# Router logits from the first norm's transposed rows and eight extra projection columns, in place of the second norm's transposes

## The reference

```python
h = patches(x) @ W_lin.T + b_lin, with class token and positions; then the text rows
h = h + attention(layernorm(h))          # Wq, Wk, Wv, causal, every fourth key left out, Wp
z = layernorm(h)
xn = z * rsqrt(mean(z * z) + 1e-5) * norm_weight
logits = xn @ router_w.T + router_b
probs = softmax(logits)
gates, idx = top_k(probs.T, T_all // 8)  # each expert picks its tokens
h = h + sum over experts of gates * (gelu(xn[idx] @ fc1.T + b1) @ fc2.T + b2) / sum of gates
```

## Time and profile before

| | |
|---|---|
| runs, median of 3 | 848.52 us (846.49 to 848.92) |
| the profiled execution | 851.07 us, span 849.0 us |
| granted TensorE clock, mean | 0.929 |
| PE busy | 748.5 us (88%), 6840 matmuls |
| PE weight loads busy | 675.5 us (80%) |
| DVE busy | 567.4 us (67%) |
| ACT busy | 398.0 us (47%) |
| POOL busy | 383.7 us (45%) |

### The profile page before, as it was taken

One profiled execution on the slowest core, in us unless ns is written; L12 is line 12 of the kernel. 1 busy time (PEld: TensorE's weight loads), 2 busy tenths in 40 slices (PEclk: granted clock), 3 DMA queues, 4 the chain that ended last, 5 costly groups with the idle time before them and its releaser, 6 DMA issues. The chain is left out here.

```text
span 849.0 us, 18781 instructions
## 1 busy us (share of the span) xinstructions
PE 748.5 (88%) x6840; PEld 675.5 (80%) x6840; DVE 567.4 (67%) x1343; ACT 398.0 (47%) x857; POOL 383.7 (45%) x534
## 2 busy tenths in 40 slices
PE   6788999999999999999999521379999999999994
PEld 5667888888888888888887421379999999999994
DVE  1245867668667677677675267785787787877561
ACT  0314445454455454454542247045547466375570
POOL 4223455364464454554542426023636437355334
PEclk9899999999999999999998755569999999999998
DMA  9965477465774566666653162112344443443122
GB/s 308 272 99 89 56 116 114 88 87 98 107 117 92 89 102 93 123 107 95 90 95 71 36 216 65 40 28 82 41 132 78 106 141 53 129 98 35 36 30 32
DMA packets 80583, 82.37 MB, mean 97 GB/s; under 512 B 35705, under 2 KB 73575, under 8 KB 80236
## 3 DMA queue, kind: packets, MB, share of 16 engines
q1 hardware_dynamic: 65964, 62.21, 37.5%
q0 software_dynamic: 11840, 11.12, 8.3%
q10 hardware_dynamic: 2688, 7.85, 3.3%
HBM read 34.59 MB, written 16.22 MB: 60 GB/s over the span
## 5 line engine op out<-in xcount | busy, mean ns | idle before, releaser
L625 POOL DMA_INDIRECT out<-r_arena x48 | 80.0, 1666 | 117.9 <-DVE r_arena L1582 106.0
L529 POOL TENSOR_SCALAR_AFFINE_SELECT r_arena<-r_arena 126x660 f32<-126x660 f32 x128 | 97.5, 771 | 59.1 <-ACT r_arena L687 58.6
L687 ACT ACTIVATE r_arena<-ps_all 126x660 f32<-126x660 f32 x128 | 92.3, 721 | 67.2 <-PE ps_all L915 66.0
L1289 DVE TENSOR_REDUCE mx<-ps_all 128x4 f32<-128x504 f32 (+1 forms) x160 | 105.0, 668 | 24.3 <-PE ps_all L892 23.1
L1300 DVE RECIPROCAL r_arena<-ps_all 128x165 f32<-128x165 f32 x64 | 76.1, 1189 | 56.3 <-PE ps_all L930 56.3
L915 PE MATMUL ps_all<-Qp,Kp 98*126 98x166 f32 x512 | 85.6, 291 | 9.9 <-DMA Qp<-mT 6.9
L892 PE MATMUL ps_all<-Kp,Qp 96*65 96x56 f32 (+1 forms) x512 | 93.5, 298 | 0.0
L1604 DVE TENSOR_TENSOR hT_lo<-r_arena,hT_hi 128x330 fp32r<-128x330 f32 x128 | 63.3, 500 | 40.3 <-ACT r_arena L794 40.3
L612 POOL DMA_INDIRECT xe<-xn_rows,r_arena x48 | 60.3, 1256 | 59.7 <-issue 35.7
L792 ACT ACTIVATE hT_hi<-ps_all,vec_s 128x330 fp32r<-128x330 f32 x128 | 69.1, 540 | 36.1 <-PE ps_all L1157 34.0
L1157 PE MATMUL ps_all<-xeT_hi,W_hi 128*128 128x330 f32 x256 | 83.4, 326 | 1.1 <-DVE xeT_lo L1596 1.1
(11 more groups left out here) (181 smaller groups left out, 1712.7 us busy)
## 6 DMA issues: line engine op xcount, KB each, us to landing
H<-w SPq DMA_DIRECT2D x16, 1024.0 KB, 5.9
Qp<-q_hi SPq DMA_DIRECT2D x64, 166.0 KB, 3.9
Kp<-k_hi SPq DMA_DIRECT2D x128, 63.0 KB, 4.1
Qp<-q_lo SPq DMA_DIRECT2D x32, 166.0 KB, 4.7
out<-H SPq DMA_DIRECT2D x16, 330.0 KB
xn_rows<-r_arena SPq DMA_DIRECT2D x16, 330.0 KB
H<-h ACTq DMA_DIRECT2D x13, 336.0 KB, 23.5
Kp<-k_lo SPq DMA_DIRECT2D x64, 63.0 KB, 4.1
```

The source lines that it names most:

```text
L529: pool.affine_select(PT[0:S, g, :, :], PT[0:S, g, :, :], [[0, 4], [STEP - 1, T]], ALU.is_ge, 0.0, base=STEP - 2, channel_multiplier=-STEP) ...
L625: pool.indirect_dma_start(rows_out, bass.IndirectOffsetOnAxis(tok[0:A, e % NTB, a:a + 1], 0), yw[0:A, a, :], None, bounds_check=NTOK - 1, ...
L687: act.activation(PT[0:S, g, :, :].rearrange("p (k h) t -> p k h t", k=2), pair[:, :, :, 0:T], ACT.Exp, scale=float(HD) ** -0.5).then_inc(e ...
L1289: dve.tensor_reduce(dst, src, AX.X, ALU.max).then_inc(max_ready, 1)
```

## The change

The logits are linear in the residual stream before its norms' scales: h after attention is (first norm's rows) / rs + bias rows + y @ Wp. G is router_w times norm_weight with each expert's mean over the 256 inputs taken away, so that the second norm's shift drops out. `route(n)` now multiplies xnT, the first norm's transposed rows of pair n, by G; it is issued in the even round, two to three rounds ahead of the projection, into unused columns of bank 2. `router_part` on DVE scales that by the first norm's spread and adds a constant, into eight columns that every token row of H gets (U). Eight columns Wp @ G are put behind the projection's weights, so `project` writes 264 columns and `residual` adds the router's part with the rest. `logits(p)` on POOL multiplies U by the second norm's scale and adds the bias. `transposes2`, `copy_xn2T` and `copy_logits` go; xn2 is still made and stored, as the experts gather it. Round 33 of PE's list goes. `router_mean`, `router_projection`, `router_bias` and their DVE parts set up the constants in rounds -1 to 1. The bank waits of `queries` and `keys` that named `copy_xn2T` or the logits now name xnT.

```diff
+DL = D + NE
 BIG0 = T - 128
 SMALL = 65
+SCRATCH = 2 * T + 6
...
-        H = sb("H", [128, NT * D])
-        H4 = H[:, :].rearrange("p (n r d) -> p n r d", n=NPAIR, r=RT)
+        H = sb("H", [128, NT * DL])
+        HL = H[:, :].rearrange("p (n r d) -> p n r d", n=NPAIR, r=RT)
+        H4, U = HL[:, :, :, 0:D], HL[:, :, :, D:DL]
...
-            W_s = sb1("W_s", [128, 4, KD, D])
...
+            W_p, W_pT = sb1("W_p", [128, KD, DL]), sb1("W_pT", [128, KD, D])
+            bpe = sb1("bpe", [128, DL])
+            bvB, bpB = sb1("bvB", [128, KD, A]), sb1("bpB", [128, KD, A])
...
+                if n >= 3:
+                    pool.wait_ge(u_ready, RT * (n - 2))
+                    apart(pool)
+                pool.tensor_tensor(spread[0:A, n % 3, :], vv[0:A, :], rs[0:A, :], ALU.mult).then_inc(spread_ready, 1)
...
+                if p == NPAIR - 1:
+                    logits(p)
                 pool.tensor_tensor(shift2[0:A, :], shift2[0:A, :], rs2[0:A, :], ALU.mult).then_inc(shift2_ready, 1)
+
+            def logits(p):
+                if p == 0:
+                    pool.wait_ge(row_in, 16)
+                    apart(pool)
+                mine = L[0:A, RT * p:RT * p + RT, :]
+                scale = rs2[0:A, :].rearrange("p (r o) -> p r o", o=1).to_broadcast([A, RT, NE])
+                bias = rb_s[0:A, :].rearrange("p (o e) -> p o e", o=1).to_broadcast([A, RT, NE])
+                pool.tensor_tensor(mine, U[0:A, p], scale, ALU.mult).then_inc(scaled, 1)
+                pool.wait_ge(scaled, p + 1)
+                apart(pool)
+                pool.tensor_tensor(mine, mine, bias, ALU.add).then_inc(logit_ready, 1)
             def norm_weight(p):
                 if p >= 2:
                     pool.wait_ge(xn_stored[p % 2], 16 * (p // 2))
                     apart(pool)
-                    pool.wait_ge(t2_done, 2 * p - 2)
...
+                if p < NPAIR - 1:
...
+                    logits(p)
...
+            act.dma_start(W_p[:, :, 0:D], watt[:, 3]).then_inc(w_in, 16)
...
+            act.dma_start(W_pT[:, :, :], wpT).then_inc(wpT_in, 16)
...
-            def copy_xn2T(p):
...
+            act.wait_ge(xn2_ready, RT * NPAIR)
...
+                if c == 0 and b >= 1:
+                    pe.wait_ge(u_ready, RT * min(b // 2 + 2, NPAIR))
+                if c == 1 and b <= 1:
+                    pe.wait_ge(router_ready, 3 + b)
...
             def project(p, r, free):
                 if r == 0:
                     pe.wait_ge(yT_ready, 4 * p + 4)
+                    pe.wait_ge(router_ready, 3)
                 pe.wait_ge(*free)
                 for k in range(KD):
-                    mm = pe.matmul(bank(project_bank(p, r))[0:A, 0:D], yT[:, p % 2, k, r * A:(r + 1) * A], W_p[:, k, :],
+                    mm = pe.matmul(bank(project_bank(p, r))[0:A, 0:DL], yT[:, p % 2, k, r * A:(r + 1) * A], W_p[:, k, :],
 ...
-            def transposes2(p, c, free):
...
-            def route(p):
-                pe.wait_ge(xn2T_ready, 2 * p + 2)
+            def router_mean():
+                pe.wait_ge(router_ready, 1)
+                for k in range(KD):
+                    mm = pe.matmul(bank(3)[:, SCRATCH:SCRATCH + NE], kf("ones")[:, 0:128], G[:, k, :],
+                                   start=(k == 0), stop=(k == KD - 1))
+                mm.then_inc(router_sum, 1)
+
+            def router_projection():
+                pe.wait_ge(wpT_in, 16)
+                pe.wait_ge(router_ready, 2)
+                for c in range(KD):
+                    for k in range(KD):
+                        mm = pe.matmul(bank(3)[:, SCRATCH + (c + 1) * NE:SCRATCH + (c + 2) * NE],
+                                       W_pT[:, k, c * 128:(c + 1) * 128], G[:, k, :],
+                                       start=(k == 0), stop=(k == KD - 1))
+                mm.then_inc(router_sum, 1)
+
+            def router_bias():
+                pe.wait_ge(bvB_ready, 1 + KD)
+                pe.wait_ge(router_ready, 3)
+                dst = bank(3)[0:A, SCRATCH + 3 * NE:SCRATCH + 4 * NE]
+                for k in range(KD):
+                    pe.matmul(dst, bvB[:, k, :], W_p[:, k, D:DL], start=(k == 0), stop=False)
+                for k in range(KD):
+                    mm = pe.matmul(dst, bpB[:, k, :], G[:, k, :], start=False, stop=(k == KD - 1))
+                mm.then_inc(router_sum, 1)
+
+            def route(n):
+                pe.wait_ge(router_ready, 2)
+                pe.wait_ge(xnT_ready, 2 * n + 2)
+                if n >= 2:
+                    pe.wait_ge(u_ready, RT * (n - 1))
+                at_col = SCRATCH + n % 2 * RT * NE
                 for r in range(RT):
                     for k in range(KD):
-                        mm = pe.matmul(bank(7)[0:A, r * NE:(r + 1) * NE], xn2T[:, k, r * A:(r + 1) * A], rw_s[:, k, :],
+                        mm = pe.matmul(bank(2)[0:A, at_col + r * NE:at_col + (r + 1) * NE],
+                                       xnT[:, n % 2, k, r * A:(r + 1) * A], G[:, k, :],
                                        start=(k == 0), stop=(k == KD - 1))
-                mm.then_inc(logit_done, 1)
+                mm.then_inc(route_done, 1)
...
-                return (xn2T_ready, 2 * (n - 2) + 2) if n >= 2 else (xnT_ready, 2 * (n + 1) + 2)
+                return xnT_ready, 2 * (n + 1) + 2
...
+                router_mean()
...
                 if has_r:
                     row_scores(m, 3, (max_ready, 5 * m + 2))
+                if b == 0:
+                    route(0)
+                    route(1)
+                    router_projection()
+                elif u == 0 and n + 1 < NPAIR:
+                    route(n + 1)
+                if b == 1:
+                    router_bias()
...
-                    route(n - 2)
...
-                    project(n - 1, 0, (k_ready, b + 3) if has_q else (logit_ready, n - 1))
+                    project(n - 1, 0, (k_ready, min(b + 3, B)))
...
-                if u == 1 and has_p:
-                    for c in range(KD):
-                        transposes2(n - 1, c, (xnT_ready, 2 * (n + 2) + c + 1) if has_t1 else
-                                    ((k_ready, v_ready)[c], b + 3) if has_q else
-                                    (resid_ready, RT * (n - 1) + 3 - c) if has_s else
-                                    ((logit_ready, n - 1), (xn2T_ready, 2 * (n - 1)))[c])
                 if has_s and b != B - 1:
                     mix_values(b, 0)
                     mix_values(b, 1)
-                if u == 1 and has_p and b != B - 1:
-                    route(n - 1)
...
+                dve.wait_ge(u_ready, RT * p + r + 1)
+                dve.tensor_tensor(HL[0:A, p, r, :], HL[0:A, p, r, :], bank(project_bank(p, r))[0:A, 0:DL], ALU.add)\
                    .then_inc(resid_ready, 1)
...
-            def copy_logits(p):
...
+            def router_rows():
+                dve.wait_ge(vec_in, 16)
+                for k in range(KD):
+                    ins = dve.tensor_scalar(G[:, k, :], rw_s[:, k, :], nwT[:, k:k + 1], None, ALU.mult)
+                ins.then_inc(router_ready, 1)
+
+            def center_router():
+                dve.wait_ge(router_sum, 1)
+                for k in range(KD):
+                    ins = dve.scalar_tensor_tensor(G[:, k, :], bank(3)[:, SCRATCH:SCRATCH + NE], -1.0 / D, G[:, k, :],
+                                                   ALU.mult, ALU.add)
+                ins.then_inc(router_ready, 1)
+
+            def router_columns():
+                dve.wait_ge(router_sum, 2)
+                for c in range(KD):
+                    ins = dve.tensor_copy(W_p[:, c, D:DL], bank(3)[:, SCRATCH + (c + 1) * NE:SCRATCH + (c + 2) * NE])
+                ins.then_inc(router_ready, 1)
+
+            def router_constant():
+                dve.wait_ge(router_sum, 3)
+                dve.tensor_copy(bpe[0:A, D:DL], bank(3)[0:A, SCRATCH + 3 * NE:SCRATCH + 4 * NE]).then_inc(router_ready, 1)
+                dve.wait_ge(router_ready, 4)
+
+            def router_part(n):
+                dve.wait_ge(route_done, n + 1)
+                dve.wait_ge(spread_ready, n + 1)
+                at_col = SCRATCH + n % 2 * RT * NE
+                for r in range(RT):
+                    dve.scalar_tensor_tensor(U[0:A, n, r, :], bank(2)[0:A, at_col + r * NE:at_col + (r + 1) * NE],
+                                             spread[0:A, n % 3, r:r + 1], bpe[0:A, D:DL], ALU.mult, ALU.add)\
+                       .then_inc(u_ready, 1)
...
+                    router_rows()
...
+                if b == -1:
+                    center_router()
+                if b == 0:
+                    router_columns()
+                if b == 1:
+                    router_constant()
+                    router_part(0)
+                    router_part(1)
+                if u == 0 and n >= 1 and n + 1 < NPAIR:
+                    router_part(n + 1)
...
-                    copy_logits(n - 1)
```

(27 more changed lines are left out.)

60 lines of the change are left out of this document (22 added, 38 removed).

## The result

The changed kernel takes 860.87 us, median of its runs (from 856.38 us), against 848.68 us for the kernel before: ratio 1.0138, 95% interval 1.0094 to 1.0182. The median counts one disturbed run of 893.72 us, which the ratio leaves out (the median of the other three is 858.74). It is slower, by some 1.3%; the forecast was 852.5 us, range 845 to 862. The profiled execution took 856.38 us with a span of 854.4, so from profile to profile it is +5.3 us, where the prediction's sum said +4.0. A later group of runs has 858.65 against 848.49 us. Most executions of the changed kernel thus cost some 10 us, twice what the two profiles show. Both numbers have to be explained.

The account below looks back on a forecast made before the run. PE was taken to bound the attention rounds, with POOL, ACT, SP and DVE level with it in places. Rounds +12.6, absorption -3.0, start +1.4 and tail -7.0 gave +4.0 us on 848.52: 852.5 us, range 845 to 862.

Parts of the forecast that it names:

- The rounds: Attention rounds: even round +1.3 us, odd round -0.4, so +0.9 a steady pair and +12.6 us over 14.
- The moved route: Even round, between two row scores on PE: the same 12 instructions and weight loads cost 1.18 us there.
- the absorption in waits for the maxima's copy: Two even rounds where PE waits for SP: the route fills these waits and low clock stays away, together -3.0 us.
- The tail: From the last pair to softmax and search: last logits need only the second norm's scale, so -7.0 us.
- The start: First rounds, with added router setup on PE and extra loads: +1.4 us in all.
- Round 0: Two routes and the router's projection, 3.1 us against a 2.26 us wait: +0.9; slow clock behind it goes, -0.7.
- The loads: Split and extra loads at the start, issued tens of us ahead; if uncovered, one more 2.16 us landing.
- (b): Odd rounds: PE's 1.3 us idle before the second value mix lowers the clock, +8 us, about 861; chance 0.2.
- (a): The forecast itself: the moved route costs more than the tail gives, 852.5 us, bounds 848 to 858; chance 0.42.
- (c): Even rounds: short PE waits for row maxima swallow 0.3 us more, a pair costs 0.6, 848.3 us; chance 0.2.
- (d): Attention rounds: PE alone is the bound, route's move free, removed transposes a gain, 831 to 835 us; chance 0.11.
- (e): The tail gives nothing, as the search waits for weights or the last xn2 rows, 859.5 us; chance 0.07.

Follow-up runs that it names:

- before_not2: Kernel before, with only one of three row tiles transposed in the second norm's transposes of pairs 0 to 14: 844.81 us, ratio 0.9966.
- the second trace: Trace of the changed kernel unaltered, run again as the standard of a later group: 858.65 us, ratio 1.0118.
- quiet kernels: The kernel before and the changed kernel, each with the loads of pairs 8 to 15 of h issued one per round: 843.15 and 849.66 us.
- fill: Changed kernel, with the route of each pair from the third on moved between the two value mixes of the odd round before: 846.28 us, ratio 0.9979.
- before_quiet: Kernel before, with the loads of pairs 8 to 15 of h issued one per round from round 0: 843.15 us, ratio 0.9927.
- quiet: Changed kernel, with the loads of pairs 8 to 15 of h issued one per round from round 0: 849.66 us, ratio 1.0032.
- spread0: Changed kernel, with round 0's 32 router instructions shared between rounds 0 and 1 and the bias moved to round 2: 864.90 us, ratio 1.0186.

## Why the prediction was right, and where it was wrong

**The rounds: right, to 0.1 us for a steady round; the sum in part by luck.** Forecast odd rounds of 12.8 us and even ones of 13.7; measured 12.71 and 13.69, a pair 26.40 against 25.66, +0.74 where +0.9 stood. The steps of the steady pair hold one by one. The second mix is released by POOL (13 waits of 1.1 us and one of 0.5) and the transposes were worth nothing in a steady pair (`before_not2`). The two operations on POOL take 0.60 us, as worked out. The moved route costs 1.10 us in place (1.18 forecast), and 87 ns per instruction by leaving 8 of 12 out; 25 ns, which the Trainium skill ("TensorE: Matmul & The Clock Gate", Back-to-back issue gap) gives for an isolated matmul and the prediction quotes, doesn't fit. What did not hold is the absorption in waits for the maxima's copy, forecast 3.0: 14 pairs at 0.74 are 10.4 us, and the rounds are 9.3 us longer, 10.1 in the second trace, so 1.1 and 0.3 us were absorbed. The two long waits went, but a new one of 1.6 us came before sample 30. That 9.3 lies so near 12.6 - 3.0 = 9.6 is luck: the pairs were put 2.2 us too high in sum, the absorption 1.9 us too high, and the two cancel.

**The tail: right.** Forecast -7.0. From the first key scores of sample 31 to the first search count the changed kernel's two traces take 25.6 us, against 33.6, 33.3 and 32.0 in the three traces that have the old tail: -6.4 to -8.0. The profile pair shows 1.8 us more, since the kernel before had 6.8 us of low clock from 452.4 us and 13.00 us in the stretch from 30 to 31, the changed kernel 3.4 us of it and 11.22, where most others have 10.2 to 10.3. That is not a gain of the change.

**The start: the mechanism half seen, the size wrong.** This is the term that failed: forecast +1.4. Two terms were in it. (1) Round 0. "32 instructions x 98 ns = 3.1 us, against a wait of 2.26 us: +0.9", and 0.7 us of low clock behind that wait saved. The instructions took 3.7 us, the clock fell during or right behind them, and 6.8 us at the lower level followed, 10.2 in the first trace. The low clock of round 1 did go, as forecast; that the new matmuls would bring one of their own was not thought of. Samples 0 to 2 take 29.8 us on average in the eight kernels with this start and these loads, against 26.0 in the two such kernels with the old one: +3.8 where 0.9 - 0.7 and 0.8 for `router_bias`, +1.0, stood. With the loads away it is 29.8 against 26.2, so it doesn't hang on them. (2) The loads. "Issued tens of us ahead of their use", and only one late landing counted as the price. What they delay isn't their own use but ACT, which issues them and then has the first norm to apply (at 28.88 us before, 29.77 in the changed kernel), and the copies of the keys, which land 2 to 3 us sooner when half of the loads are away. The first key scores of sample 0 come at 64.7 us on average in the eight, 60.8 in the two: +3.9 where +0.4 stood. In the quiet kernels the difference is 1.4 to 1.7. That loads and issues set this start is shown by the two quiet kernels; that 256 KB and two issues more make 3.9 us rather than 1 to 2 is an average over few traces with 6.4 us between the extremes, and stays open in its size.

With +7.7 for +1.4 the sum is 4.0 + 6.3 = 10.3 us, and the later group of runs has 10.2. So close a match is partly chance, as +7.7 is a difference of averages over traces that differ by several us. The change costs 10 us, not 4; that its time still lies in the range of 845 to 862 is owed in part to the room left there for the clock rival (b). The first profiled execution of the changed kernel had an early start (61.85 us, the lowest of its kind), the kernel before's own a slow stretch of clock near the end; that is why the profiles differ by only 5.3 us and looked like the forecast.

**The rivals.** (a) happened, with a start added to it that lifts it out of its own bounds of 848 to 858. (b) gives its number, 861, by accident: its mechanism didn't occur at the 1.1 us pauses of the changed kernel, with the clock at 1.00 through the rounds, and at a pause 0.7 us longer it occurs in two of thirteen. The low clock that did cost time stood in round 0. (c) had 0.6 us a pair, and 0.74 lies midway between it and the forecast's 0.9; it fell with the rounds as a whole, 9.3 us longer where 8.4 - 3.0 = 5.4 was its sum. (d) fell with `before_not2`, (e) with the tail.

## What to carry to other kernels

Work moved to another place of a balanced schedule is paid where it lands, not where it was: look for the pause that the removal leaves, and put it there (`fill`, 12 us less than with the route in the even round, which brings the change level with the kernel before). Count DMA issues as work of the engine that makes them: an engine that has computing to do early should issue only the loads that are wanted early (`before_quiet` and `quiet`, -5 and -9 us). And compare stretches between fixed marks over several traces before taking the difference of two spans for the effect: here each span had 2 to 3 us of its own.

## What the runs showed that was not expected

- The granted clock fell with PE fully busy: 3.41 us busy of 3.41, most of it matmuls of eight columns, and then 10.2 us at 0.50. Nine more traces with these 32 matmuls in a row show the fall, for 6.8 us. Twelve such matmuls between wide ones, in 14 even rounds, were followed by no fall, and neither were 12 and 20 of them in two rounds (`spread0`). The Trainium skill ("TensorE: Matmul & The Clock Gate", HAM oscillation — how this bites in real kernels) puts the oscillation down to waits between groups of matmuls; in this kernel waits of 1.13 to 1.73 us were followed by it in some cases and not in most, and this row of small matmuls without any wait.
- An issue of a load of one pair of h (336 KB) on ACT's queue took 0.5 us for the first ones, up to 3.99 us later, and 1.7 us on average over thirteen.
- From the search's first count to the end, code that no kernel changed takes 350.9 to 356.0 us; why is not explored.
